# A selective-scan decoder layer: the next row's first scans and six step sizes moved ahead of the expert input, its transposes and the routing

## The reference

```python
x = x + mamba(_layernorm(x))          # selective scan: D_INNER 512, D_STATE 16
x = x + cross_attention(_layernorm(x), ctx_1024)
x = x + moe(_layernorm(x))            # 8 experts, 2 of them per token
```

## Time and profile before

| | us |
|---|---|
| median of 3 runs | 1504.59 (1502.41 to 1505.41) |
| the profiled execution, its own time | 1504.71 |
| its span | 1502.9 |
| VectorE busy | 1327.0 (88%) |
| TensorE busy | 1218.4 (81%) |
| ScalarE busy | 999.3 (66%) |
| GpSimd busy | 949.9 (63%) |
| scans, 192 + 64 | 438.1 + 146.1 |
| mean granted clock of TensorE | 0.927 |

### The profile page before, as it was taken

How to read it: one execution, slowest core, us unless ns; L and a number is a source line. 1 busy time by engine, 2 the same in 40 slices (tenths; PEclk the granted TensorE clock), 3 DMA queues, 4 the chain that set the end, 5 groups by cost and what they waited for, 6 DMA issues and landing times. The chain is left out here.

```text
span 1502.9 us, 22669 instructions
## 1 busy us (share of the span) xinstructions
PE 1218.4 (81%) x6134; PEld 853.0 (57%) x6134; DVE 1327.0 (88%) x1744; ACT 999.3 (66%) x1475; POOL 949.9 (63%) x522
## 2 busy tenths in 40 slices
PE   5978887689788888899788888899677777786897
PEld 2446664575555555685555555586355455575565
DVE  5479999888999999988899999988999999974687
ACT  5755554447978878837877877837777777732654
POOL 1379998514799889614798988723598988731000
PEclk9989998699899999999799999999789989897799
DMA  8112231421222212422121222512111112210111
GB/s 258 65 63 57 84 95 32 142 85 59 71 56 71 74 59 91 157 71 80 50 78 56 83 65 70 175 46 80 47 60 47 59 57 62 89 57 29 57 57 56
DMA packets 88013, 114.54 MB, mean 76 GB/s; under 512 B 9964, under 2 KB 62965, under 8 KB 87934
## 3 DMA queue, kind: packets, MB, share of 16 engines
q1 hardware_dynamic: 83836, 110.86, 23.5%
q10 hardware_dynamic: 4098, 2.74, 0.6%
HBM read 88.85 MB, written 24.73 MB: 76 GB/s over the span
## 5 line engine op out<-in xcount | busy, mean ns | idle before, releaser
L1827 DVE TENSOR_TENSOR_SCAN work<-ps,work 128x1024 f32<-128x1024 f32 x192 | 438.1, 2283 | 27.0 <-ACT ps L1299 24.9
L2413 PE MATMUL ps<-ident,work 128*128 128x128 f32 x1536 | 296.1, 314 | 163.4 <-DVE stage L1875 56.0
L1299 ACT ACTIVATE ps<-dt,a_neg 128x1024 f32<-128x1024 f32 x256 | 284.9, 1116 | 124.8 <-DVE work L1827 81.4
L2413 PEld LDWEIGHTS ps<-ident,work 128*128 128x128 f32 x1536 | 187.0, 156 | 287.4 <-DVE stage L1875 113.3
L887 POOL TENSOR_TENSOR work<-dtu,b_bc 128x1024 f32<-128x1024 f32 x124 | 290.2, 2369 | 44.4 <-PE ps L2413 43.2
L1875 DVE SCALAR_TENSOR_TENSOR stage<-ps,c_tok,stage 128x512 f32<-128x512 f32 x360 | 254.4, 733 | 9.7 <-PE ps L2413 8.2
L2435 PE MATMUL ps<-w,work 128*128 (+1 forms) x1024 | 250.0, 389 | 2.8 <-DVE work L2009 2.0
L2435 PEld LDWEIGHTS ps<-w,work 128*128 128x128 f32 x1024 | 195.9, 196 | 40.4 <-issue 4.1
L2385 PE MATMUL ps<-nfT,w 128*128 128x512 bf16 x512 | 163.6, 415 | 26.0 <-DVE work L1945 14.6
L887 POOL TENSOR_TENSOR work<-dtu,w_out 128x1024 f32<-128x1024 f32 x64 | 149.3, 2353 | 40.4 <-PE ps L2413 40.4
L906 POOL TENSOR_TENSOR stage<-stage,work 128x512 f32<-128x512 f32 x120 | 150.2, 1275 | 37.8 <-ACT work L1322 37.8
(11 more groups left out here) (189 smaller groups left out, 1921.8 us busy)
## 6 DMA issues: line engine op xcount, KB each, us to landing
b_bc<-b_rows SPq DMA_DIRECT2D x32, 512.0 KB, 4.8
w_out<-b_rows SPq DMA_DIRECT2D x32, 512.0 KB, 4.5
wbc<-combine_rows SPq DMA_DIRECT2D x64, 256.0 KB, 4.0
work<-z_rows SPq DMA_DIRECT2D x8, 1024.0 KB, 7.6
dtu<-conv_rows SPq DMA_DIRECT2D x12, 512.0 KB, 6.3
conv_rows<-mix SPq DMA_DIRECT2D x20, 256.0 KB, 2.8
stage<-in_x SPq DMA_DIRECT2D x8, 512.0 KB, 5.5
z_rows<-mix SPq DMA_DIRECT2D x16, 256.0 KB, 2.8
```

Source lines behind the costliest of these rows:

```text
L1299: act.activation(decay_in(d, alone, opening), dt[:, d, :], ACT.Exp, scale=a_neg[:, bass.ds(it * 2 + (d * N + hf * (N // 2) + par), 1)]).th ...
L1827: dve.tensor_tensor_scan(h, decays, h, 0.0, ALU.mult, ALU.add).then_inc(scan_done, 1)
L2413: mm = pe.transpose(ps[:, a % HT_BANKS, d * P:(d + 1) * P], slot(par, d)[:, a * P:(a + 1) * P], ident[:, :])
```

## The change

Four places of the code are written in another order: the lists that set the order of banks, and the stretch on ScalarE, VectorE and TensorE. GpSimd's and SyncE's code stays. No instruction is added or removed.

```diff
-                        both("N")[0:2] + [("ZL", 1, 0)] + both("N")[2:4] + steps[4:5] + [("G", 0, 0)] + steps[5:] + [("TN", 0, 0), ("C", 0, 0)] +
+                        steps[4:6] + both("N")[0:2] + [("ZL", 1, 0)] + both("N")[2:4] + [("G", 0, 0)] + steps[6:] + [("TN", 0, 0), ("C", 0, 0)] +
...
-        dve_between = (both("Y") + both("O") + both("Q") + both("V") + steps[0:4] + [("G", 0, 0)] + steps[4:7] +
+        dve_between = (both("Y") + both("O") + both("Q") + both("V") + steps[0:6] + [("G", 0, 0)] + steps[6:7] +
...
                     opening_decay(0)
+                    softplus(3)
+                    softplus(4)
                     experts_in(0)
+                    act.wait_ge(scan_done, b * N * CT + 1 + SCAN_CREDIT)
+                    opening_decay(1)
+                    softplus(5)
                     if r > 0:
                         keep_left(1)
-                    softplus(3)
                     experts_in(1)
-                    softplus(4)
-                    act.wait_ge(scan_done, b * N * CT + 1 + SCAN_CREDIT)
-                    opening_decay(1)
-                    gap_exponential()
-                    softplus(5)
                     if n_row is not None:
                         norm_row(n_row, 0)
+                    gap_exponential()
                     softplus(6)
...
                     step(0)
-                    expert_input(0)
                     mean_square(1)
+                    step(1)
                     if n_row is not None:
                         norm_stats(ph, 0, xn_a, 0, n_row)
-                    step(1)
-                    expert_input(1)
                     step(2)
                     opening_scan(0)
+                    expert_input(0)
                     step(3)
-                    route_scores(ph)
+                    expert_input(1)
                     step(4)
+                    opening_scan(1)
                     if n_row is not None:
                         row_shift(n_row, 0)
+                        norm_stats(ph, 0, xn_a, 1, n_row)
+                    step(5)
+                    route_scores(ph)
+                    opening_scan(2)
                     route_ranks(ph)
-                    step(5)
-                    opening_scan(1)
-                    if n_row is not None:
-                        norm_stats(ph, 0, xn_a, 1, n_row)
                     step(6)
                     last_input(6)
                     take_c()
...
                     last_input(7)
-                    opening_scan(2)
                     opening_scan(3)
...
-                do_all(ph, steps[0:4])
+                do_all(ph, steps[0:6])
                 do_all(ph, tiles_of("N", 0))
                 if r > 0:
                     do(ph, "ZL", 1, 0)
                 do_all(ph, tiles_of("N", 1))
-                do(ph, *steps[4])
                 do(ph, "G", 0, 0)
-                do_all(ph, steps[5:])
+                do_all(ph, steps[6:])
```

## The result

The changed kernel takes 1534.3 us (median of 4 runs, 1531.81 to 1536.92), the kernel before 1505.0 in the same comparison. The ratio is 1.0191, interval 1.0169 to 1.0213: slower by 29 us. That is the upper end of the range (1512 to 1534): the median lies 0.3 us above it, while the ratio on the 1504.7 that the forecast started from gives 1533.4. The forecast itself was 1524. The profiled execution has a span of 1535.1 us, 32.2 more than before; it is the slowest of the four.

What follows compares the result with a forecast made beforehand. VectorE was taken to bound the kernel, 194.55 of 200 us busy in the loop. 1504.7 + 19.2 (three stretches) + 1.5 (clock) - 1.5 (loop's give-back) = 1523.9, said as 1524 us; range 1512 to 1534.

Steps and rivals of the forecast that it cites:

- Early part: VectorE, first stretch: statistics moved behind step 1, scan 0 starts 2.1 us and scan 1 3.9 us earlier.
- G behind the copies: TensorE, first stretch: gate product G awaits ScalarE's copies into `nfT`, at 372.5 instead of 365.37, TensorE idle about 3.5 us.
- Scan 2's wait: VectorE, first stretch: scan 2 reached at 377.0, waits 3.4 us for decay 2, with ranks and later steps queued behind.
- Decay 3: ScalarE, first stretch: behind the shift and `norm_row(1)`, at 388.6 instead of 381.21; the loop's first scan 7.4 us later.
- The sum of the three stretches: Lateness of the three stretches between rows: 7.4, 6.8 and 5, together 19.2 us.
- the +5: Third stretch: scan 3 6.6 us late, `route_weights` 5.9 us if blocked or 3.2; so 3.9 to 6.6 late, 5 taken.
- 0.5 a stretch for the clock: TensorE may run slower behind its pause ahead of G: 0 to 2.9 us per stretch, 0.5 each taken, +1.5.
- 0 for the blocking: VectorE's CAST of `route_scores` may be held to the end of GpSimd's product: 0 to 1.2 us, 0 taken.
- Give-back: Loop behind each stretch makes up delay from VectorE's 3% idle: at most 1 or 2 us, 0.5 each taken, -1.5.
- the rival of the partial cover: Stretch's end absorbs half the sum, since early scans let GpSimd and transposes run ahead: 1514, chance 0.14.
- The rival of the halved clock: TensorE's pause drops it to 1.2 GHz for S6 and S7 in all three stretches: 1532, chance 0.15.
- The other side: Early scans decide: scan 1 3.9 us sooner, no wait at scan 2, perhaps 1 us gained per stretch: 1502, chance 0.06.

Runs made afterwards that it cites:

- e1: Changed kernel with scan 2 of the opening moved back on VectorE behind the input of step 7; ratio 1.0085 to the kernel before.
- e3: Changed kernel with three idle products filling TensorE's pause ahead of G; ratio 1.0165 to the kernel before.
- e10: Changed kernel with the last copies into `nfT` ahead of softplus 5 and `gap_exponential` behind decay 2 on ScalarE; ratio 1.0092 to the kernel before.
- e6: Changed kernel with the last copies into `nfT` ahead of softplus 5, `gap_exponential` behind softplus 6 and scan 2 behind step 7; ratio 1.0052 to the kernel before.
- e2: Changed kernel with `gap_exponential` moved behind softplus 6 on ScalarE; ratio 1.0186 to the kernel before.
- e4: Changed kernel with both `gap_exponential` behind softplus 6 and three idle products ahead of G; ratio 1.0142 to the kernel before.
- e11: Changed kernel with copies ahead of softplus 5, `gap_exponential` behind decay 2, scan 2 behind step 7, `route_weights` ahead of step 7; ratio 1.0024 to the kernel before.
- e9: Kernel before with `route_weights` on VectorE ahead of step 7 in all three stretches; ratio 0.9993 to the kernel before.
- e5: Changed kernel with the last copies into `nfT` ahead of softplus 5 and `gap_exponential` behind softplus 6; ratio 1.0117 to the kernel before.

## Why the prediction was right, and where a term was off

Direction and mechanism held, by the trace and by e1, e3 and e10. The size was too small: 19.2 us in the three stretches against 26.6, and 19 against 29 in the time. That the time still came to the end of the range, and not beyond it, is luck.

- Early part: scan 1 at 23.7 us behind S0 against 27.9 (forecast: 369.25, so 24.0). VectorE's wait ahead of step 1 is there (1.47). Ahead of step 2 it doesn't wait, as the forecast had it: the last operation of the statistics is held by the first product (1.88), and scan 0 comes at 14.65 behind S0, 0.5 later than forecast. e6 shows that the early part isn't free: with the two repairs 7.7 us are left, some 1.1 of them by the clock in the first stretch. Which of its moves costs how much no run separates.
- G behind the copies: forecast from 372.5 to 373.0, measured 372.87, S0 standing 0.66 later. Right. The pause ahead of it was 3.0 to 3.1 us in all three, forecast 3.5, 3.0 and 2.9.
- Scan 2's wait: forecast 3.4 us, measured 3.61, and 3.56 and 4.88 in the other stretches. What stands behind it is the larger half: e1 regains 13.7 us by moving it.
- Decay 3: forecast 388.6, measured 390.28 at S0 + 44.4, so 1.0 later than forecast relative to S0.
- The sum of the three stretches was 7.4 + 6.8 + 5, measured 8.4 + 7.7 + 10.5. Two terms were mis-sized, and the third stretch is most of it.
- In the first two stretches, 1.0 and 0.9: softplus 6 was forecast at 32.0 us behind S0 and stands at 33.1. S6 was to end at 31.3, and ends near 33, since S6 and S7 took 2.1, 1.6 and 1.8 us longer; the gap was to be ready at 31.8, and is ready at 32.7, since the last subtraction of the scores took 1.47 instead of 0.17 beside GpSimd's product. The forecast took 0.5 a stretch for the clock and 0 for the blocking. With either wait left softplus 6 starts at 32.8 to 33.0 (e2, e3), with both gone at 31.1 and 31.6 (e4). e4 takes the whole gap away; what the blocked subtraction is worth by itself no run shows.
- In the third stretch, 5.5: scan 3 ended 8.2 late instead of 6.6, and these 1.6 are what e3 regains there with the clock up. The other 3.9 are the weights: the +5 assumed some 4.3 us for them, its upper end the 5.9 of before, and they took 8.2. So the upper end of that term was no bound: the weights were blocked for longer than before, by three products instead of two.
- Give-back, -1.5: none seen. The first two loops take 0.7 and 0.1 us more than before, not less; nor does anything speak for the rival of the partial cover (1514).
- The rival of the halved clock gave 1532, nearest to the measured 1534.3, and it isn't the cause: its price was 2.9 us per stretch for S6 alone, and the clock is worth 0.3, 0.3 and 1.6 by itself, and at most 1.9 with the gap gone. Its number fitted because the weights of the third stretch (3.9) and the blocked subtraction, which it didn't have, stood in for most of that price.
- The Trainium skill's rule on the shared ports ("SBUF — State Buffer", "SBUF: two separate sides") agrees here: the CAST waited for the step input that ran (1.23), and the next instruction with two SBUF inputs, the subtraction, for the product (1.47). In the third stretch the CAST met the product itself (2.13), as forecast, and the subtraction took 0.17. In the first two the forecast looked only at the CAST.
- The Trainium skill's rule on the clock ("TensorE: Matmul & The Clock Gate", "What's actually happening"), that the halved rate is the default and activity releases it, agrees with e3: with the pause filled, the clock stays at 1.00. That filling the pause pays by itself, which one may read from it, e3 doesn't bear out in the first two stretches.
- The other side (early scans pay) is out by e11 against e9, and by e10, which meets its condition: S6 is on time and VectorE doesn't wait at scan 2 in the first two stretches, yet the yardstick is 48.1 where this rival's sum gives 42.9 to 44.4. That sum went along VectorE alone; in e10 decay 3 stands 40.9 us behind S0 in the first stretch, behind the shift and `norm_row(1)`.

What stays open: the medians differ by 29.3 us, the stretches by 26.6. The 2.7 us between them are within the spread of single runs, and the comparison of the fourteen profiles above gives them to no part of the change.

## What to carry to other kernels

An instruction moved ahead in an in-order queue is worth nothing if what it needs comes late; as scan 2 did here, it then holds everything behind it, and the price is read from the first thing behind it that another engine waits for. Before moving one, follow its latest input back through the other engines' queues in the new order, and include the small waits such as the gap. Two waits of equal length hide each other: remove them singly and together. And a small VectorE operation beside long GpSimd products took up to one product's time here (2.33 us for 128x8 elements, a product 2.33 to 2.35); its place matters more than its size.

## What was not expected of the hardware

- A subtraction of 128x8 elements on VectorE took 0.17 us with GpSimd idle and 1.47 beside its product; a TENSOR_SCALAR of 128x4 took 0.17 and 1.88; the six small instructions of the weights took 2.2, 5.9 and 8.2 us, by what GpSimd ran.
- TensorE's code was the same in the first stretch of e5, e6 and e10, and so were its pauses of about 1 us: it was at 1.2 GHz behind them in one profile (e6) and at 2.4 in the others (e5, e10). That stretch of e6 was 1.1 us longer than expected. What decides it no run shows.
